# Cross-attention and a routed feed-forward block: attention cut into nine stages of two batches, and some mask and context work moved from VectorE to GpSimd

## The reference, cut to what matters

```python
x = x + xattn(layernorm(x), ctx, ctx, mask, Wq, Wk, Wv, Wo)   # 16 batches x 128 tokens x 128, 16 heads of 8
x = x + ffn(layernorm(x), wg, w1, w3, w2)                     # 8 experts of 256, top 2, softmax weights

# xattn: scores = Q K^T / sqrt(8); masked keys get -1e9; softmax over keys; times V; times Wo
# ffn:   logits = x wg^T; the two best experts; y = w2[e] (silu(w1[e] x) * (w3[e] x)); weighted sum
```

## Time and profile before

| | us |
|---|---|
| median of 3 runs (lowest, highest) | 294.29 (292.64, 297.12) |
| profiled execution, its own time | 292.38 |
| its span in the trace | 290.6 |
| busy: PE, DVE, ACT, POOL | 211.9, 211.0, 137.2, 91.6 |

### The profile page before, as it was taken

The page is one execution under the profiler, slowest core; times in us unless marked ns, Lnnn a source line. Parts: engine busy times, 40 slices in busy tenths (PEclk is TensorE's granted clock), DMA queues, the critical chain, the costliest instruction groups (busy, mean ns, idle before and its releaser), DMA issues.

```text
span 290.6 us, 5041 instructions
## 1 busy us (share of the span) xinstructions
PE 211.9 (73%) x1381; PEld 154.3 (53%) x1381; DVE 211.0 (73%) x618; ACT 137.2 (47%) x293; POOL 91.6 (32%) x104
## 2 busy tenths in 40 slices
PE   0767897898959978769654867677959999988010
PEld 0543564566636555547432644366848899877010
DVE  4689956598737978389778776548897888867095
ACT  5799138364735548234215665324434555544000
POOL 4311200040003010101545366211546564656740
PEclk9995559799978999595965685559999999999655
DMA  6934402332052111320315511240242232221537
GB/s 216 340 103 107 114 11 52 74 90 59 9 117 64 41 29 37 83 59 1 89 48 169 173 39 46 57 101 0 54 101 67 76 91 68 80 76 34 166 82 218
DMA packets 24793, 24.99 MB, mean 86 GB/s; under 512 B 3806, under 2 KB 19168, under 8 KB 24382
## 3 DMA queue, kind: packets, MB, share of 16 engines
q1 hardware_dynamic: 21502, 18.37, 25.2%
q0 software_dynamic: 2688, 5.48, 5.8%
q10 hardware_dynamic: 576, 0.82, 0.9%
HBM read 12.31 MB, written 6.31 MB: 64 GB/s over the span
## 4 chain that ended last, share of the span: by engine, by line
PE 39%; DVE 29%; DMA 14%; issue 8%; ACT 5%; SPq 3%; POOL 1%; POOLq 0%; DVEq 0%; ACTq 0%
DVE m_neg L1405 6%; DMA ys<-big 5%; PE bank L545 5%; PE bank L669 4%; DMA bd<-st 4%; PE bank L704 4%; PE bank L690 4%; PE bank L551 3%; PE bank L769 3%; DMA big<-ys 2%; DVE st L1349 2%; PE bank L743 2%; SPq L434 2%; PE bank L575 2%; PE bank L770 2%
## 5 line engine op out<-in xcount | busy, mean ns | idle before, releaser
L1405 DVE TENSOR_REDUCE m_neg<-bank 128x4 f32<-128x512 f32 x64 | 43.4, 684 | 22.2 <-PE bank L704 22.1
L1047 POOL DMA_INDIRECT ys<-big x39 | 38.1, 976 | 37.9 <-DVE big L1441 23.0
L932 ACT ACTIVATE big<-bank 128x512 f32<-128x512 f32 x64 | 37.3, 597 | 26.3 <-PE bank L690 25.5
L704 PE MATMUL bank<-bd,st 128*128 128x512 f32 x64 | 32.9, 544 | 11.5 <-DMA bd<-st 11.0
L690 PE MATMUL bank<-bd,st 128*128 128x512 f32 x64 | 33.9, 550 | 4.9 <-ACT big L932 3.3
L1013 POOL DMA_INDIRECT xg<-rows,rows_i x24 | 24.1, 1004 | 33.3 <-DVE rows_i L1214 14.2
L997 POOL TENSOR_SCALAR ve<-mv 128x4 f32<-128x4 f32 x8 | 1.8, 226 | 100.8 <-DVE mv L1076 100.8
L807 ACT ACTIVATE st<-bank 128x128 fp32r<-128x128 f32 (+1 forms) x78 | 22.3, 329 | 21.5 <-PE bank L756 15.7
L1349 DVE SCALAR_TENSOR_TENSOR st<-st_hi,cst,bank 128x512 fp32r<-128x512 f32 x32 | 22.9, 747 | 10.4 <-ACT st_hi L904 10.4
L769 PE MATMUL bank<-bd,st 128*128 x78 | 22.9, 315 | 8.8 <-DVE big L1441 8.7
L904 ACT ACTIVATE st_hi<-bank,cst 128x512 fp32r<-128x512 f32 x32 | 21.8, 690 | 10.2 <-PE bank L545 9.9
(11 more groups left out here) (169 smaller groups left out, 467.0 us busy)
## 6 DMA issues: line engine op xcount, KB each, us to landing
bd<-st SPq DMA_DIRECT2D x62, 104.0 KB
big<-xg SPq DMA_DIRECT2D x39, 64.5 KB, 1.8
raw<-in_L_ffn_w SPq DMA_DIRECT2D x2, 1024.0 KB, 7.0
x_all<-in_x SPq DMA_DIRECT2D x4, 256.0 KB, 4.2
rows<-in_mask_BxS_if POOLq DMA_DIRECT2D x4, 256.0 KB, 5.1
ctx_all<-in_L_ffn_w SPq DMA_DIRECT2D x1, 1024.0 KB, 4.9
ctx_all<-in_ctx SPq DMA_DIRECT2D x3, 256.0 KB, 4.8
raw<-ys SPq DMA_DIRECT2D x3, 256.0 KB, 4.6
```

The costliest lines, as they stand in the source:

```text
L704: nc.tensor.matmul(s1[k % s1_ring(u)][:, :].rearrange("p (j q) -> p j q", j=NJ), st[:, u % 2, 0, b - 1, g, :], bd_slot(1, n)[:, g, :, :], ...
L932: nc.scalar.activation(prob[n % 2][:, NJ * g:NJ * (g + 1), :].rearrange("p h q -> p (h q)"), s2[k % 2][:, :], ACT.Exp, scale=SCALE).then_i ...
L1047: pool.indirect_dma_start(ys, bass.IndirectOffsetOnAxis(xt[n % XR][:, D:RW].bitcast(I32), 0), y_sb[n % YR], None, bounds_check=PAIRS - 1, ...
L1405: nc.vector.tensor_reduce(m_neg[:, H * (b - 1) + g:H * b:NG], s1[k % s1_ring(u)][:, :].rearrange("p (j q) -> p j q", j=NJ), X, ALU.max, ne ...
```

## The change

The loop runs over `p` = 0 to 8, stages of two batches. The stacks of stage `p + 1` are made in stage `p`, so that SP copies their key diagonals a whole stage before the scores by query that read them; SP's order in a stage is maxima rows of `p - 1`, key diagonals of `p + 1`, query diagonals of `p`. A stack unit holds two groups of heads of two batches, so a matmul has 256 columns instead of 512 and there are twice as many. A stage has 11 ticks: scores by query in ticks 0 to 7, scores by key of the stage before in ticks 3 to 10 (`LEAD = 3`). Maxima are rounded, transposed and copied eight times instead of four. GpSimd, not DVE, makes the mask tables and the context remainders of quartets 1 to 3 and clears the second value buffer. Routing and weight pieces have new ticks.

```diff
+LEAD = 3
+TICKS = 2 * NG + LEAD
+WEIGHT_STEPS = {(7, 0): [0], (7, 1): [1], (7, 2): [2], (7, 4): [3], (8, 1): [4], (8, 2): [5], (8, 5): [6], (8, 6): [7]}
+UNITS = [(1, 0), (1, 1), (0, 0), (0, 1)]
...
+            def stack_unit(p, k):
+                is_k, h = UNITS[k]
...
+                for i in range(2):
+                    g = 2 * h + i
...
+                        last = split_product(half, parts, (by_batch(x_hi[:, columns_of]), by_batch(x_lo[:, columns_of])))
...
+            for p in range(NP + 1):
+                front, tail = p + 1 < NP, p >= 2
...
+                for t in range(TICKS):
+                    if t < 2 * NG and p < NP:
+                        scores_by_query(p, t)
...
+                    if t >= LEAD and p >= 1:
+                        scores_by_key(p - 1, t - LEAD)
...
+                    if t == 8 and p >= 1:
+                        values(2 * (p - 1))
...
+            diagonals(1, 0)
+            for p in range(NP + 1):
+                if p >= 1:
+                    maxima_rows(p - 1)
+                if p + 1 < NP:
+                    diagonals(1, p + 1)
+                if p < NP:
+                    diagonals(0, p)
...
+                if p == 0:
+                    for k in range(2, 6):
                         clear_diagonal(k)
+                if p == 1:
+                    for k in range(6, 8):
+                        clear_diagonal(k)
...
+            for u in range(1, NQ):
+                masks(u)
                 if u + 1 < NQ:
+                    load_mask(u + 1)
+                mask_context(u)
+                inverse_deviation(u)
+                context_rest(u)
...
+                    if p == 7 and t == 4:
+                        second_statistics(2)
+                    if p == 7 and t == 8:
+                        normalise(2 * QB, NQ + 2)
+                    if p == NP:
+                        if t in (2, 3, 4):
+                            routing_step(2, t - 2)
+                        if t == 8:
+                            place_rows(2)
```

More of the change, by code:

```diff
@@ L52 @@
 NQ = B // QB
+NP = B // 2
 T = QB * S
@@ L151, in slot_order @@
         if name[0] == "st":
-            bank = STACK_BANKS[name[-1] % 4]
+            bank = stack_banks(name[1])[name[2]]
             alternate = 0
@@ L659, in values @@
+                last.then_inc(work_full, 1)
             def values(n):
@@ new lines, in _ @@
+            for k in range(4):
+                stack_unit(0, k)
+            for p in range(NP + 1):
+                front, tail = p + 1 < NP, p >= 2
+                n = 2 * (p - 2)
+                if front:
+                    stack_unit(p + 1, 0)
+                if p >= 1:
+                    transpose_maxima(p - 1)
+                if tail:
+                    heads_by_query(n)
+                if front:
+                    stack_unit(p + 1, 1)
+                if tail:
+                    values(n + 1)
+                    heads_by_dim(n)
+                if front:
+                    stack_unit(p + 1, 2)
+                if tail:
+                    project_out(n)
+                if front:
+                    stack_unit(p + 1, 3)
+                if tail:
+                    heads_by_query(n + 1)
+                for t in range(TICKS):
+                    if t < 2 * NG and p < NP:
+                        scores_by_query(p, t)
+                    if t == 1 and tail:
+                        heads_by_dim(n + 1)
+                    if t >= LEAD and p >= 1:
+                        scores_by_key(p - 1, t - LEAD)
+                    if t == 3 and tail:
+                        project_out(n + 1)
+                    if t == 8 and p >= 1:
+                        values(2 * (p - 1))
+                    for name in fills(p, t):
+                        if name[0] == "xT":
+                            transpose_tokens(name[1])
+                        elif name[0] == "V":
+                            context_values(name[1])
+                        else:
+                            fill(name)
@@ L944, in _, with tokens_high, context_high, take_values @@
-            take_heads(B - 1)
+            def tokens_high(u):
+                full(("xT", u))
+                copy(x_hi[:, :], work_bank(("xT", u))[:, :]).then_inc(xhi_ready, 1)
+            def context_high(u):
+                act.wait_ge(ck_ready, u + 1)
+                copy(ck_hi[:, :], ck[:, :]).then_inc(ckhi_ready, 1)
+            def take_values(u):
+                full(("V", u))
+                if u >= 2:
+                    act.wait_ge(o_full, QB * (u - 1))
+                else:
+                    act.wait_ge(va_cleared[u], 1)
+                src = work_bank(("V", u))[:, :].rearrange("p (m i j d) -> p m i j d", i=2, j=NJ, d=HD)
+                dst = va[u % 2].rearrange("p (m i j) r -> p m i j r", i=2, j=NJ)
+                for i in range(2):
+                    last = copy(dst[:, :, i, :, HD * i:HD * (i + 1)], src[:, :, i, :, :])
+                last.then_inc(into_sbuf(("V", u)), 1)
@@ new lines, in stack_high, with probabilities @@
+            def stack_high(p, k):
+                n = 4 * p + k
+                full(("st", p, k))
+                if n >= SH:
+                    before = n - SH
+                    taken(act, ("st", before // 4, before % 4))
+                one = C_ONE_K if UNITS[k][0] else C_ONE
+                nc.scalar.activation(st_hi[:, n % SH, :], work_bank(("st", p, k))[:, :], ACT.Identity, bias=cst[:, one:one + 1]
+                                     ).then_inc(sthi_ready, 1)
+            def probabilities(p, i):
+                k = 2 * NG * p + i
+                n, g = divmod(k, NG)
+                act.wait_ge(s2_full, k + 1)
+                if g == 0 and n >= 2:
+                    act.wait_ge(o_full, n - 1)
+                nc.scalar.activation(prob[n % 2][:, NJ * g:NJ * (g + 1), :].rearrange("p h q -> p (h q)"),
+                                     s2[k % 2][:, :], ACT.Exp, scale=SCALE).then_inc(prob_ready, 1)
```

648 lines of the change are left out of this document (285 added, 363 removed), and 3 rows, old and new, of the table FILLS.

## The result

The changed kernel takes 299.67 us (median of 4 runs, 297.84 to 300.52) against 293.47 (4 runs beside it): ratio 1.0225, 95% interval 1.0141 to 1.031. It is slower; whether by 2%, the interval leaves open. The forecast was 290.0 with a range of 280 to 301; the time lies inside the range, on the other side of no change.

A forecast was written before the change was run, and what follows sets the result against it. VectorE's order up to the placing of quartet 2's rows was taken to gate the end. Terms -0.7 - 11.6 - 2 + 11.7 + 1 - 1 = -2.6 from 292.38 gave 289.8, rounded to 290 us, range 280 to 301.

The forecast's parts named there:

- the price of the stage changes: VectorE's idle time at stage boundaries: five at 3.7 us against four at 1.7 before, +11.7 us, between +6 and +18.
- Five at 3.7: Changes into stages 1 to 5: scores by key, values, last exponential, head copy and rounding precede VectorE's first stack, 3.7 us each.
- Holes: VectorE's three waits for diagonal transfers before the first reductions of rounds 1 to 3 go: -11.6 us.
- The low clock and the ticks: Part of PE's low clock behind the holes goes, saving VectorE idle time in two tick stretches: -2, between nothing and 10.4.
- first rival: PE's clock stays up without holes, all 10.4 us of idle time in two tick stretches go: 281.4 us, chance 0.28.
- Work on VectorE: Up to the placing of quartet 2's rows: -6.3 moved off, +3.8 and +1.8 added, sum -0.7 us, between -2 and +0.5.
- Matmuls of 256 columns: Stacks on PE: twice as many matmuls at half width cost nothing, since PE is ahead of ScalarE and VectorE.
- Start: Before stage 1: first diagonals about 2 us earlier, but clearings stand ahead of other work; net +1 us, between -2 and +4.
- GpSimd: Masks and remainders moved to GpSimd: some 3.5 us more per quartet, early in a stage, costing nothing; mask operation 0.42 to 1.28.
- The gate: Feed-forward start waits for quartet 2's placed and scattered rows; last quartet's statistics now precede the scatter wait: -1.0, between -2.5 and 0.
- The second: Rival: routing late at three stage changes, about 3 us each, placing 9 us later and after 176: 299 us, chance 0.22.
- The third: Rival: ten new large GpSimd operations each hold a VectorE one by 0.97 us: +9.7, 299.5 us, chance 0.07.

The follow-up runs named there:

- e2: Changed kernel with the tanh of quartets 0 and 1 moved behind the last exponential and head copies: runs of 289.21, 295.26, 295.45 and 916.82 us.
- e14: e13 with the tanh of quartets 0 and 1 moved behind the last exponentials: 292.71 us, 0.9929 of the kernel before.
- e9: Changed kernel without the third product of the stacks (low weights times high data): median 297.11 us, 0.9926 of the kernel before.
- e11: Changed kernel with values, heads and projections of stages 2 to 6 moved from the change into the ticks: 293.76 us, 0.9976 of the kernel before.
- e1: Changed kernel with masks, context remainders and the second clearing given back from GpSimd to VectorE: 299.65 us, 1.0296 of the kernel before.
- e13: e11 with stage 7's heads also in its ticks and quartet 2's second statistics and row normalising later: 294.21 us, 0.9982 of the kernel before.
- e15: e14 with half of quartet 1's scatters ahead of quartet 2's inverse deviations in GpSimd's queue: 288.59 us, 0.9838 of the kernel before.
- e5: Changed kernel with the third stack of a change ahead of a batch's values and heads on PE and ScalarE: 300.33 us, 1.0263 of the kernel before.

## Why the prediction was wrong

**The step that failed** is in the price of the stage changes: "There are eight; into stages 6, 7 and 8 the routing that stands behind the eighth reduction fills it. So five at 3.7 against four at 1.7." The three forecast at nothing have 3.13, 4.51 and 5.26 us of idle time, 12.9 in all. The routing did fill VectorE, but while it did, the others did not go on: ScalarE stood at the tanh that waits for the routing's end, and when VectorE was free the heads began (e2 takes 1.4 and 3.0 us off the changes into 6 and 7; with the heads in the ticks as well, e14 has 2.6 left of the 8.0 into 7). In the change into stage 8 no tanh waits, and VectorE's own part ends early; its waits for PE and ScalarE are in the timeline above, but no run took them away alone, so which queue sets that change is open. I took work on one engine for cover without following the queues of the other two.

**The size of the other changes.** Five at 3.7 were 3.72, 4.66, 4.51, 3.49 and 4.52, or 2.4 more. I had the amount nearly right for a wrong reason: I costed a tail of scores, exponential and rounding, while the changes into 2 to 5 are a row of PE's values, heads, projections and stacks, 7.1 to 8.5 us of PE's work (e9, e11). What the kernel before has left without its holes was 11.5 and not 6.8, which lowers the difference by 4.7. Together 11.7 became 22.3.

**Holes: right.** No score by query waits for a transfer after stage 0; -11.6, where the earlier trace rows had the three.

**The low clock and the ticks: too small, and not the clock.** -2 was taken between 0 and -10.4; VectorE's idle time fell by 3.9 in the ticks and by 2.9 in the last stretch. The range held it, my choice inside it was poor. It is not the first rival's gain: the granted clock did not stay up, it was 1.00 in the changes into stages 2 to 6 but 0.62 to 0.85 in the ticks of these stages, against 0.78 to 0.90 in the ticks of rounds 1 to 3 before. What shortened the idle time in the ticks is not shown.

**Work on VectorE: a small miss.** The durations sum to 140.4 us up to the placing against 140.1, +0.4 where -0.7 was forecast, with GpSimd's holds of 1.6 among them. Busy time rose by 1.2, as the operations overlap less (15.2 us against 16.0).

**Matmuls of 256 columns: right in price.** They mostly follow one another every 0.12 us, and those of 512 columns before every 0.23. That the stacks stay ahead of ScalarE was wrong: ScalarE waits 15.6 us for PE ahead of 24 of the 32 stacks, against 9.9 before, and that cover is what a change no longer has.

**Start: too small to tell.** VectorE's idle time there rose by 2.0, but its work fell by 1.8, and the first reduction came at 24.16 instead of 23.93, where +1 was forecast. Among the changed kernels that leave the start as it is, it came between 22.2 and 24.8.

**GpSimd: right as far as seen.** Undoing its part gained no time (e1). A comparison of the mask takes it 1.51 us, outside my bounds of 0.42 and 1.28.

**The gate: right, its size by luck.** The first tile waits for the gather behind the scatters, as I had it. It is -1.0 from the placing to the first tile, as forecast, but in all the changed kernels but e13 the tile follows the placing by 15.9 to 17.6 us, and the 17.4 of before lies within that: a single -1.0 shows nothing of the statistics that I had put it down to.

**The rivals.** The first, the clock staying up, did not come. The second, "the routing comes late at the change of stage", gave 299 and decided at a placing after 176: the time is 299.67, the placing 177.31. Its size was right; of its place and its mechanism, half. The three changes it names have 12.9 us of VectorE's idle time, and those into 1 to 5 together have 9.4 more than the four before, holes aside. I had VectorE late and PE waiting for it, and found VectorE idle, waiting for heads behind ScalarE's tanh. At 0.22 it was too low, since the trace of before already held the argument: these operations are a serial chain that now crossed three changes. The third, GpSimd holding VectorE, is refuted as the cause: four held operations cost about 1.6 us, not 9.7, and undoing the move gave no time.

## What to carry to other kernels

A hole that an engine fills is cover only for that engine: at a change of stage, walk through the queue of each engine in order and look for an instruction that waits for the fill (here a tanh of 0.23 us that held 2.6). Cutting stages finer to hide transfers repeats everything that stands at the boundary; before halving a stage, move what can stand between other work, as heads and values did before, out of the boundary, and then the finer stages pay (0.984 in e15, which also has the tanh late and GpSimd's same work in another order).

## What the runs showed of the hardware

GpSimd holding VectorE, at the change into stage 1 of the changed kernel (timelines of GpSimd and of VectorE):
```profile
31.04 1.27 POOL L1064 TENSOR_TENSOR ck_lo<-ck,ck_hi 128x512 fp32r<-128x512 f32 x1 [2.35 <-ACT ck_hi L827]
32.28 1.51 POOL L1056 TENSOR_SCALAR nokeep<-rows 128x512 fp32r<-128x512 int32 x1
...
31.65 0.70 DVE L1207 CAST m_hi<-m_neg 128x32 fp32r<-128x32 f32 x1
32.38 0.54 DVE L1208 COPY m_hl<-m_hi 128x32 f32<-128x32 f32 x1
```
The first operation, 0.18 us elsewhere (at 97.77), ends at 32.35 with GpSimd's remainder (32.31). The second, 0.18 elsewhere too, ends 0.9 us ahead of GpSimd's comparison, so it was held for part of it only. Two pairs of layer-norm operations took 0.98 and 0.96 instead of 0.59, beside the remainders at 60.43 and 94.39. The Trainium skill's "Advanced Engine Details and Errata", section "VectorE Performance Modes", has GpSimd and two-port VectorE operations block each other on a shared SBUF port. By that rule more holds were to come with more work on GpSimd; these rows agree, at a price of 0.36 to 0.52 us each, 1.6 in all, where I had 0.97 each.

The change into stage 8 is the same work in the changed kernel, e2, e5, e9 and e11. It took 10.88 and 10.89 us where the granted clock was 0.50 (e2, e11), and 8.82, 8.68 and 8.49 at 0.84, 0.87 and 0.89. In the ticks ahead of it PE had been busy 8.66 of 10.75 us in the changed kernel, at 0.50, and 6.68 of 10.72 in e2, at 0.74: of the two, the one that had the higher clock ahead was at the lower level in the change. What decides it was not settled; a gain of 2 us ahead of such a stretch can be lost in it.
